# Gathered queries pass through SBUF: ScalarE copies them out of PSUM, VectorE multiplies in place

## What is computed

```python
xp = xn + (xn @ Wpos + bpos + deg * Wdeg + bdeg)      # xn = layernorm(x)
q, k, v = (xp @ Wq + bq), (xp @ Wk + bk), (xp @ Wv + bv)          # 8 heads of 16
att = einsum('ehd,ehd->eh', q[dst], k[src]) / 4        # one score per edge and head
att = nan_to_num(clip(att, -50, 50))
alpha = softmax of att over the edges that share a dst
aggr = segment_sum(v[src] * alpha, dst)
x = x + aggr @ Wo + bo
x = x + gelu(layernorm(x) @ W1 + b1) @ W2 + b2
```

## Time and profile before

| | |
|---|---|
| runs | 2732.53, 2742.39, 2750.90 us |
| the profiled execution | 2747.29 us, span 2745.3 us, mean granted TensorE clock 0.739 |
| busy: PE, PEld | 1663.2 us (61%), 1456.9 us (53%) |
| busy: POOL, DVE, ACT | 1487.1 us (54%), 1452.9 us (53%), 912.1 us (33%) |
| DMA | 322.97 MB moved, mean 118 GB/s |

### The profile page before, as it was taken

How to read it: one execution, slowest core, us unless ns; L and a number is a source line. 1 busy time by engine, 2 the same in 40 slices (tenths; PEclk the granted TensorE clock), 3 DMA queues, 4 the chain that set the end, 5 groups by cost and what they waited for, 6 DMA issues and landing times.

```text
span 2745.3 us, 44122 instructions
## 1 busy us (share of the span) xinstructions
PE 1663.2 (61%) x11693; PEld 1456.9 (53%) x11694; DVE 1452.9 (53%) x2484; ACT 912.1 (33%) x1616; POOL 1487.1 (54%) x1584
## 2 busy tenths in 40 slices
PE   7555555656666767666544565555656666665645
PEld 5454554555555656554533454555555555655644
DVE  9654444445555555555464444445455555555544
ACT  3223222223443444343232222222333443433422
POOL 0445555555555555556635555555655555655663
PEclk9668777667887777778566777767787777777776
DMA  2433334344433434444423333333433333443443
GB/s 67 132 108 121 112 109 125 115 121 122 125 115 116 127 115 127 124 123 141 132 79 104 120 106 119 117 117 120 131 119 119 117 117 117 123 128 117 129 136 93
DMA packets 120300, 322.97 MB, mean 118 GB/s; under 512 B 31459, under 2 KB 43684, under 8 KB 120170
## 3 DMA queue, kind: packets, MB, share of 16 engines
q0 software_dynamic: 75072, 205.10, 26.0%
q1 hardware_dynamic: 44292, 115.07, 12.5%
q10 hardware_dynamic: 838, 1.60, 0.2%
HBM read 313.45 MB, written 9.73 MB: 118 GB/s over the span
## 4 chain that ended last, share of the span: by engine, by line
DVE 25%; another core or an unknown queue 22%; issue 20%; PE 17%; DVEq 11%; ACT 3%; ACTq 1%; DMA 0%; SPq 0%
PE ps L1332 7%; PE ps L1350 6%; DVE dots L1079 6%; DVE prod L1069 5%; DVEq L354 4%; DVEq L388 3%; DVE hot L987 2%; DVE msg L1101 2%; DVE acc L982 1%; DVE q_parts L834 1%; DVEq L982 1%; DVE not_nan L1081 1%; DVEq L987 1%; ACT dist L697 1%
## 5 line engine op out<-in xcount | busy, mean ns | idle before, releaser
L561 POOL DMA_INDIRECT kv<-kv_tab,src_idx x1564 | 1483.3, 948 | 1230.9 <-PE ps L1350 541.0
L1350 PE MATMUL ps<-msg,hot 128*128 128x136 f32 x3896 | 764.3, 367 | 425.6 <-DVE acc L982 232.9
L1350 PEld LDWEIGHTS ps<-msg,hot 128*128 128x128 f32 x3896 | 705.6, 267 | 484.0 <-issue 298.0
L1332 PE MATMUL ps<-q_parts,hotT 128*128 x5844 | 560.0, 265 | 526.9 <-DVE prod L1069 228.5
L1332 PEld LDWEIGHTS ps<-q_parts,hotT 128*128 x5844 | 483.0, 121 | 610.7 <-issue 591.8
L1069 DVE TENSOR_TENSOR prod<-kv,ps 128x1024 f32<-128x1024 f32 (+1 forms) x198 | 238.2, 1203 | 362.1 <-remote 286.1
L987 DVE SCALAR_TENSOR_TENSOR hot<-dst_col,neg_base,ps 128x1024 f32<-128x1024 f32 (+1 forms) x246 | 311.7, 1267 | 126.1 <-issue 124.6
L700 ACT ACTIVATE hotT<-dist 128x1024 bf16 x246 | 259.9, 1057 | 331.2 <-remote 291.5
L697 ACT ACTIVATE dist<-dst_rows,neg_node 128x1024 bf16<-128x1024 int32 x246 | 282.5, 1148 | 153.0 <-issue 146.3
L1101 DVE TENSOR_TENSOR msg<-kv,ps 128x1024 f32<-128x1024 f32 (+1 forms) x198 | 238.7, 1205 | 105.5 <-issue 72.4
L706 ACT ACTIVATE msg<-att 128x64 f32<-128x64 f32 (+1 forms) x198 | 49.7, 251 | 625.9 <-DVE att L1084 468.9
(11 more groups left out here) (215 smaller groups left out, 1000.8 us busy)
## 6 DMA issues: line engine op xcount, KB each, us to landing
dst_rows<-in_dst SPq DMA_DIRECT2D x194, 512.0 KB
kv<-kv_tab,src_idx POOLq DMA_INDIRECT x1564
kv_tab<-qkv SPq DMA_DIRECT2D x25, 128.0 KB
kv_tab<-qkv SPq DMA_DIRECT2D x3, 768.0 KB
out_tab<-z SPq DMA_DIRECT2D x24, 64.0 KB
out<-out_tab SPq DMA_DIRECT2D x1, 1498.5 KB
hot<-in_L_gnn_W SPq DMA_DIRECT2D x2, 256.0 KB
w<-in_L_gnn_W SPq DMA_DIRECT2D x2, 256.0 KB
```

Of the source, the lines that this page charges most:

```text
L561: pool.indirect_dma_start(kv[:, u, c, :], None, kv_tab[l][:, :], bass.IndirectOffsetOnAxis(ap=src_idx[:, c, at(g)], axis=0)).then_inc(kv_i ...
L1332: last = MM(qd[:, c * P:(c + 1) * P], hotT[:, bass.ds(pr % 2, 1), c * P:(c + 1) * P], q_parts[:, at(t), k * D:(k + 1) * D], start=first an ...
L1350: last = MM(agg, hot[:, u % 2, c, :], msg[:, u % 2, c, :], start=(c == 0), stop=(c == nch - 1))
```

## The change

ScalarE gets one more instruction per group, `copy_q`: it waits until the gather of the group is complete, copies `qd` from PSUM into `prod` in SBUF, and raises `q_copied`. VectorE's product now reads keys and `prod`, both in SBUF, and writes back to `prod`. TensorE's gather of the next group waits for `q_copied` in place of `prod_done`. In ScalarE's order the copy of g + 1 stands behind the exponentials of g and ahead of the one-hots of g + 2.

```diff
+        q_copied = sems("q_copied")
...
+                def copy_q(g, b):
+
+                    act.wait_ge(hotT_used[l], b + 2)
+                    full = chunks_of(g) * P
+                    nc.scalar.activation(prod[:, 0:full], qd[:, 0:full], ACT.Copy).then_inc(q_copied[l], 1)
...
                 one_hots(word, 0, 0, 0)
                 if l == 0:
                     fold_kept(1)
+                copy_q(0, word(0)[0])
                 one_hots(word, 1, 1, 0)
...
                     if even and runs(slot, 1):
                         log_and_exp()
+                    if not isinstance(g, int) or g + 1 < NG:
+                        copy_q(g + 1, word(d + 1)[0])
                     if not isinstance(g, int) or g + 2 < NG:
                         one_hots(word, d + 2, r, n)
...
-                    dve.wait_ge(hotT_used[l], b + 2)
+                    if isinstance(g, int) and g == NG - 1:
+                        dve.wait_ge(hotT_used[l], b + 2)
+                    dve.wait_ge(q_copied[l], g + 1)
                     nc.vector.tensor_tensor(prod[:, 0:full].rearrange("p (c d) -> p c d", d=D), kv[:, u, 0:nch, 0:D],
-                                            qd[:, 0:full].rearrange("p (c d) -> p c d", d=D), ALU.mult).then_inc(prod_done[l], 1)
+                                            prod[:, 0:full].rearrange("p (c d) -> p c d", d=D), ALU.mult).then_inc(prod_done[l], 1)
...
                 def gather_q(u, g, a, b, shift):
...
                     if not (isinstance(g, int) and g == 0):
-                        pe.wait_ge(prod_done[l], g)
+                        pe.wait_ge(q_copied[l], g)
...
                 def tail_biases():
...
-                    pe.wait_ge(prod_done[l], NG)
+                    pe.wait_ge(q_copied[l], NG)
```

## The result

| | before | after |
|---|---|---|
| median of 10 runs, us | 2743.01 | 2729.97 |
| lowest to highest, us | 2732.5 to 2752.2 | 2716.4 to 2741.9 |
| profiled span, us / mean granted clock | 2745.3 / 0.739 | 2734.8 / 0.748 |

The ratio is 0.9948, with a 95% interval of 0.993 to 0.9966: 13 us less, no change by the bound of 1%. I had forecast 2837 us, slower. Beside two later series of runs on other chips the same pair gave 1.0037 [1.0011, 1.0062] and 0.9965 [0.9932, 0.9999], and the kernel before run against itself gave 1.0027 [1.0007, 1.0046]. So 0.3% between two kernels tells nothing here, and the change is best called neutral, -14 to +10 us.

The account below looks back on a forecast made before the run. No engine is full, so waits decide: POOL's burst of 8 indirect DMAs plus a rest sets 11.74 us a group. 2747 + 56 + 38 = 2841 us, median 2837; range 2690 to 2925, the forecast's own 2780 to 2895.

Parts of the forecast that it names:

- The wait taken away brings nothing: TensorE's gather: its 228.5 us wait for the product goes, but the new wait for the copy ends no sooner.
- as laid out (4.1): Late group: copy starts at 1315.60; after copy and one-hot on ScalarE the next gather begins at about 1319.7.
- The copy, 1.02 us, 0 on the path: ScalarE: 198 copies of 1018 ns delay 88 products by about 1.06 us; 0 on the path, upper bound 93 us.
- Two SBUF operands hold POOL's issues, 94 us: POOL issues starting during the product are held until it ends: 56 us in 88 waiting groups, 38 us in 110 others.
- All of it lengthens bursts, and each burst's end is what releases the next step.: POOL's bursts: the 56 and 38 us of held issues count in full towards the kernel's time.
- the 1.8 to 2.1 us behind a burst: Late group: VectorE's and POOL's waits end this long after the burst's last issue; burst plus this rest gives 11.74 us.
- the 0.64 forecast: Late group: the burst's second issue is held by the product and ends at 1318.71, not 1318.07, 0.64 us later.
- the signs that I had named: Wrong if POOL's issues stay at 946 ns or product starts that wait fall well below 88.
- The period of 12.4 us: Late groups: the time of one group rises to about 12.4 us in place of 11.74.
- 88: Groups in which VectorE's product waits for the gather (69 + 19); a count well below would show the prediction wrong.
- no change: Chance 0.17: product seldom holds an issue, or savings like those of "Faster" balance it; 2715 to 2770, about 2747 us.
- Faster: Chance 0.20: after further tiles' sums, gathers without the product wait are seen before the burst closes; 2694 us, 2600 without contention.

Follow-up runs that it names:

- Taking the lead back: Changed kernel, with TensorE's gather waiting for the previous group's product again, copy and two-SBUF product kept: 2734.7 us, 0.9963 of before.
- the lead alone: Kernel before, with a second pair of PSUM banks for odd groups' queries, so 84 of 198 gathers wait one product less, without copy: 1.0000.
- T: Series of runs on the chip of S, in which TensorE's completions are seen at once; the kernel before took 2100.6 us.
- the copy alone: Changed kernel in T, gather waiting for the product again and product's second operand lane numbers in PSUM: 2182.0 us, 1.0384 of before.
- copy and lead without held issues: Changed kernel, product's second operand lane numbers in PSUM instead of copied queries: 2787.7 us, 1.0138 of before; in T 2138.9 us, 1.0183.
- Held issues alone: Kernel before, product's second operand from the values' half of the kv buffer in SBUF instead of queries in PSUM: 0.9965, repeated 0.9963.
- pauses: Kernel before, POOL clearing a scratch buffer (0.54 us) after each burst's first issue (early, 0.9943) or ahead of its seventh (late, 0.9959).
- S: Series of runs on another chip, with before, change, early pause and one-hots first side by side; before 2673.7 us, change 1.0037.
- one-hots first: Changed kernel, ScalarE's one-hots of group g + 2 ahead of the copy of g + 1 instead of behind: 1.0294 of before, in S 1.0279.

## Why the prediction was wrong, step by step

*The wait taken away brings nothing:* right where completions are held. The gather's wait moved to `hotT`, 332.7 us in 103 places, and at 1274.69 it starts 3.84 us after the copy did, about as laid out (4.1). Taking the lead back (0.9963 against 0.9948, intervals that overlap) and the lead alone (1.0000) agree. In T it is worth 43 us beside the copy.

*The copy, 1.02 us, 0 on the path:* the duration was right (1013 ns). The zero is not shown. In T the copy alone costs 81 us. With completions held, no run had the copy without the lead and without held issues; copy and lead without held issues cost 1.38% there, 38 us, and with them nothing. Whether those 38 us are the copy's stays open.

*Two SBUF operands hold POOL's issues, 94 us:* the size was right. The issues that start inside a product, more than 0.13 us before its end, are 154; the rule gives 87.5 us for them and their measured lengthening is 88.2; the group's busy time grew by 93.4. The Trainium skill's sentence ("SBUF — State Buffer", "Who interferes with whom") that two SBUF inputs contend with GpSimd agrees with this, and its inference for `tensor_tensor` does not: 948 against 1008 ns.

***The step that failed* is the one behind it: "All of it lengthens bursts, and each burst's end is what releases the next step."** What releases the next step comes about 11.7 us after the burst's start, whether issues were held or not: 11.66 us without and 11.78 with. So 150 held issues cost some 150 x 0.12 = 18 us by this estimate instead of 88, and 44 completions now come inside a burst and let 22 bursts follow without a wait, where there were 6. Held issues alone gave 0.9965 and 0.9963, pauses 0.994 and 0.996. I had read the 1.8 to 2.1 us behind a burst as a constant added to its length; in these kernels it is mostly what is left of a span counted from the burst's start. The span is not fixed to the last: with held issues alone, bursts in which one of the first three was held are 10.52 us long and are seen 12.09 us after their start, against 9.71 and 11.62 without, so there 0.47 of 0.81 us comes through.

By stage, the step was nearly right where I had laid it out. The late groups have 12.30 and 12.17 us (first and second layer), against 11.78 and 11.89 before: 0.3 to 0.5 us of the 0.64 forecast. It failed in the others: nothing was lost up to product 36 (in S 19.5 us were), and there was a gain where steps of finished tiles are interleaved. So none of the signs that I had named could catch the miss. The period of 12.4 us nearly came, the issues are at 1008 ns, and the waiting products are 86 against 88.

*The rivals:* "no change" came in, but by neither of its two reasons: the product does hold issues, and the other savings were not the lead's. "Faster" named the right place, a gather seen before the burst closes over it; the run without the lead, with 38 completions inside bursts, shows that it comes from the held issue.

What stays open: why a completion waits for the burst's end at all, why not in T, whether the recording has part in it, and what the change costs in T.

## What to carry to other kernels

When an engine idles a similar time after every burst of another, test with a pause in the burst whether the idle time is added to the burst or is the remainder of a fixed span; only in the first case does lengthening the burst cost its length. An interference can be predicted to within 1% in busy time and still have the wrong price, so write down beside each added busy time which wait would shrink. And run the kernel before anew beside every experiment: its own time moved from 2748 to 2101 us between series, while the instructions of POOL and VectorE took as long as ever in the kernels profiled.

## What the hardware showed that I had not expected

- TensorE's completions can stay unseen until a burst of 8 indirect DMAs is over (206 of 249 gathers late in the kernel before at 2743 us, 3 of 246 with copy and lead in T, where the kernel before took 2101). VectorE's are not held in the same bursts: `att` ends at 1275.08, and ScalarE, which waits for it, starts at 1275.11.
- They are not locked, but come later and later. In the kernel before, in the burst from 679.55 to 689.24, the last matmul of line 1310 ends at 683.18 and is seen at 683.20, that of line 1294 ends at 684.02 and is seen at 685.22, that of line 1320 at 684.86 and 686.68, that of the gather at 686.20 and 691.34. That looks like a queue which drains slowly while POOL issues; this is argued, not shown.
- In that time TensorE also slows: 20 gather matmuls in 1.58 us, then single ones, 1.4 us from start to start (1286.53, 1287.98).
- A gap of 0.4 to 0.8 us within the first three issues of a burst lets completions of gathers and sums through inside it (38 to 60 instead of 1); a gap after the sixth issue gave 9.
- Completions come inside bursts also where nothing is held but TensorE has its gather earlier (the lead alone: 19). Many of them alone do not make a kernel fast: one-hots first, which has held issues too, had 68 and 70 and took 1.03 of the kernel before.
